# A recurrence stage of the prefix tiles issued right after its inputs instead of inside the next tile's gate stage

## The reference

```python
xn = _layernorm(x, axis=-1)
x = x + _L0_attn_ref(xn, ...) + _L0_ffn_ref(xn, ...)

# attention, 4 heads, 256 key and 512 value columns a head, per chunk:
g = log_sigmoid(xn @ Wgk1 @ Wgk2 + bgk2) / 16
bc = cumsum(g)                         # inside the chunk
qg = q * exp(bc) * scale ; kd = k * exp(-bc)
o  = tril(qg @ kd.T) @ v + qg @ S
S  = S * exp(b_last) + (k * exp(b_last - bc)).T @ v   # carried from chunk to chunk
o  = o * rsqrt(mean(o*o)) * rms_w * silu(xn @ Wg) ;  out = o @ Wo

# experts: 4 of them, the two with the best gate score are mixed per row
h = relu(_layernorm(xf @ w1 + b1)) ; y = _layernorm(h @ w2 + b2)
```

## Time and profile before

| | us |
|---|---|
| time, median of 2 runs | 2794.62 (both 2794.62) |
| time of the profiled execution | 2792.33 |
| its span on the slowest core (core 1) | 2790.8 |
| spans of all cores | 2765.2 to 2790.8 |
| PE busy | 1543.2 |
| DVE busy | 951.6 |
| ACT busy | 881.0 |
| POOL busy | 107.6 |

### The profile page before, as it was taken

How to read it: one execution, slowest core, us unless ns; L and a number is a source line. 1 busy time by engine, 2 the same in 40 slices (tenths; PEclk the granted TensorE clock), 3 DMA queues, 4 the chain that set the end, 5 groups by cost and what they waited for, 6 DMA issues and landing times.

```text
span 2790.8 us, 25315 instructions; the slowest of 8 cores (2765.2 to 2790.8 us)
## 1 busy us (share of the span) xinstructions
PE 1543.2 (55%) x6272; PEld 583.4 (21%) x6272; DVE 951.6 (34%) x2139; ACT 881.0 (32%) x1617; POOL 107.6 (4%) x152
## 2 busy tenths in 40 slices
PE   1390347316389245656965953089435656966850
PEld 0040013101134112212322311034211212322310
DVE  2433234232511233331363254430233332253253
ACT  1411361127213322313533532223413222533531
POOL 1000000000000000001010000000000000000000
PEclk9595578758699678877987975599768787988975
DMA  8041404240044310005554625223410104534323
GB/s 125 0 76 30 77 1 67 43 73 1 15 58 76 55 23 16 16 16 89 93 100 74 107 38 114 68 44 48 72 27 16 23 16 68 99 65 86 54 38 120
DMA packets 258284, 155.31 MB, mean 56 GB/s; under 512 B 173016, under 2 KB 242648, under 8 KB 258144
## 3 DMA queue, kind: packets, MB, share of 16 engines
q0 software_dynamic: 84576, 94.96, 21.6%
q1 hardware_dynamic: 168960, 41.96, 8.4%
q10 hardware_dynamic: 4608, 16.78, 1.8%
HBM read 198.04 MB, written 8.39 MB: 74 GB/s over the span
## 4 chain that ended last, share of the span: by engine, by line
PE 49%; DVE 20%; DMA 11%; issue 8%; ACT 7%; SPq 2%; DVEq 2%; ACTq 0%; POOL 0%; POOLq 0%
PE pa L291 20%; PE pb L291 19%; PE pf L291 7%; DVE s_bb L546 4%; DMA s_kgT<-s_kgs 4%; DVE s_kgs L668 2%; DMA s_gx<-x_tm 2%; DMA s_ogf<-s_ogc 2%; SPq L405 2%; ACT s_sg L470 2%; DVEq L64 2%; PE pd L291 1%; PE pc L291 1%; DVE s_z L928 1%; DVE s_z L934 1%
## 5 line engine op out<-in xcount | busy, mean ns | idle before, releaser
L291 PE MATMUL pa<-s_w,s_xn 128*128 128x512 bf16 x1280 | 328.0, 402 | 388.9 <-DVE s_v L638 236.8
L291 PE MATMUL pb<-s_w,s_xn 128*128 128x512 bf16 x1280 | 314.0, 390 | 3.9 <-DMA s_w<-W 3.9
L291 PEld LDWEIGHTS pa<-s_w,s_xn 128*128 128x128 bf16 x1280 | 124.0, 101 | 557.2 <-issue 434.7
L291 PE MATMUL pf<-s_w,s_ogf 128*128 128x512 bf16 x512 | 147.0, 458 | 123.2 <-DMA s_ogf<-s_ogc 123.2
L291 PE MATMUL pa<-s_w,s_hfm 128*128 128x512 bf16 x512 | 128.2, 396 | 74.5 <-DMA s_hfm<-s_h 64.6
L767 ACT ACTIVATE s_jb<-s_ogc 128x512 bf16<-128x512 bf16 x64 | 40.3, 629 | 394.1 <-DVE s_ogc L761 392.1
L291 PEld LDWEIGHTS pb<-s_w,s_xn 128*128 128x128 bf16 x1280 | 123.0, 100 | 165.6 <-issue 37.8
L546 DVE TENSOR_TENSOR_SCAN s_bb<-c_os,s_bb 128x128 f32<-128x128 f32 x256 | 108.8, 425 | 107.0 <-ACT s_bb L539 81.1
L848 DVE TENSOR_TENSOR s_mcol<-s_scol 128x8 f32<-128x8 f32 x16 | 2.7, 168 | 403.4 <-ACT s_jb L908 402.8
L291 PE MATMUL pb<-s_w,s_hfm 128*128 128x512 bf16 x512 | 123.0, 383 | 0.0
L668 DVE TENSOR_SCALAR s_kgs<-s_kd,s_eb 128x128 bf16<-128x128 bf16 x256 | 65.2, 255 | 167.4 <-DMA s_kgT<-s_kgs 108.8
(11 more groups left out here) (176 smaller groups left out, 2287.4 us busy)
## 6 DMA issues: line engine op xcount, KB each, us to landing
s_w<-W POOLq DMA_DIRECT2D x32, 1024.0 KB, 12.8
s_w<-Wv_p POOLq DMA_DIRECT2D x8, 1024.0 KB, 16.8
s_w<-Wv POOLq DMA_DIRECT2D x8, 1024.0 KB, 14.2
s_w<-Wg POOLq DMA_DIRECT2D x8, 1024.0 KB, 11.4
s_w<-Wo POOLq DMA_DIRECT2D x8, 1024.0 KB, 10.9
s_gx<-x_tm ACTq DMA_DIRECT2D x16, 512.0 KB, 4.2
out<-s_jf ACTq DMA_DIRECT2D x16, 512.0 KB, 2.9
s_xt<-xp_tm POOLq DMA_DIRECT2D x4, 1024.0 KB, 10.9
```

Of the source, the lines that this page charges most:

```text
L291: ret = e.matmul(out=o, lhsT=l, rhs=r, start=st, stop=sp)
```

## The change

DE of a prefix tile is no longer kept for the next tile's stage B. It is issued at the end of its own loop iteration, behind C of its tile and behind A of the next one, and so ahead of the small loads and of all of B of the next tile. `pend_pDE[0]` stays `None`, so the call of `emit_pend_pDE` in `emit_pend_G` does nothing. No operation is added or removed.

```diff
@@ -1138,7 +1138,7 @@
         cpar = cpar_of[("p", st)]
         pv = wu_next(Wv_p[:, 0:512])
         gw_ = load_B_smalls((Wgk1_p, Wgk2_p, bgk2c_p), gate=False)
-        r_ = stage_B(gw_, gate=False, xnm=xnm, epar=cpar, mid=emit_pend_pDE)
+        r_ = stage_B(gw_, gate=False, xnm=xnm, epar=cpar)
         eqm, emm = r_
         tpms, qbm_, kbm_ = stage_C(True, eqm, emm, pre=(pv, None), epar=cpar)
         sqw = [(ve, ve.n)]
@@ -1149,7 +1149,7 @@
         blks = [stage_A_blk(nsrc, nt0, b, ncp, (), sq_w=sqw)
                 for b in range(NBLK)]
         xnm = stage_A_xpose(blks, (te, te.n))
-        pend_pDE[0] = (tpms, cpar)
+        stage_DE(True, tpms, epar=cpar)
     pend_G = [None]
```

## The result

The changed kernel takes 2764.44 us (median) against 2794.68 in the same comparison. The ratio of the two is 0.9887, 95% interval 0.9874 to 0.9901, so 28 to 35 us are gained, about 1.1%. The forecast was 2765. The interval leaves out 1, so the gain is clear of the noise; under the 2% that was set as the bound, it counts as no change.

A forecast was written before the change was run, and what follows sets the result against it. The chain was half PE, otherwise split, with no engine the bound everywhere. Gains of 16.8 + 12.0 = 28.8 us off 2792.33 gave 2763.5, plus 2.3 for the median 2765.8; forecast 2765, range 2755 to 2778.

The forecast's parts named there:

- small loads: Loads ahead of B's first matmuls, now waiting for DE and lying open: 5.2 us at one place, 5.9 at the other.
- second place: DE inside B of the first main tile, with the expert gate: Ln at 682.3 against 694.3, 12.0 us gained.
- 16.8 us: Gain predicted inside B of the second prefix tile: Ln starts at 369.7 against 386.5.
- first place: DE inside B of the second prefix tile: moved ahead, it covers the wait for the transposes; 16.8 us gained.
- Ln: Activation behind DE and B's Sigmoids, taken as the mark: each us it comes earlier is a us off the end.
- cold clock: Rival: TensorE stays at 1.2 GHz in DE, 9 us more at each place, 2784; chance 0.06.
- row of the same loads: Trace row pricing the small loads' landing at 3.7 us, used instead of the skill page's about 2.0 us.
- V's quarters: Last three quarters of V's weights, issued about 344 instead of 291, landing by 365, needed at 430; costed at nothing.
- first rival: Small loads land late, sharing DMA engines with three 1 MB loads: 16.8 instead of 3.7 us, 2792; chance 0.07.
- cold groups of 3.4 and 2.7 us: Times taken for the first and second wgk1 groups on TensorE in B, behind the small loads.
- bounds of 27 to 33 us: Range of the whole gain from the bounds on small loads and second wgk1 group: 2761 to 2767.
- 24.7 us: Gain inside B of the second prefix tile from transposes ending in DE's shadow, before the price of the small loads.

The follow-up runs named there:

- e4_hold: The kernel before, DE not moved, with the second to fourth quarters of V's weights held until the transposes of xn landed; ratio 0.9833, 47 us gained.
- e3_smalls: The changed kernel with the small loads, and the first weight quarters ahead of them, issued ahead of DE; ratio 0.9827 to the kernel before.
- e8_tail: The changed kernel with V's quarters held, DE reordered by key block, its last items behind stage A and small loads ahead of them; 2662.64 us, ratio 0.9513.
- e5_after_hold: The changed kernel with V's second to fourth weight quarters held until the transposes have landed; 2745.62 us, ratio 0.9820 to the kernel before.

## Why the prediction was right, and where it saw too little

Step by step, times on the slowest core; at the second place the prediction's times are shifted by the 16.8 us that it gave to the first.

| step | predicted | measured |
|---|---|---|
| first place: first diagonal | 292.4 | 292.45 |
| DE's last copy ends | 341.3 | 342.1 |
| first matmul behind the small loads | 346.5 | 347.2 |
| second wgk1 group ends | 352.6 | 353.4 |
| Ln | 369.7 | 370.1 |
| second place: DE's last copy ends | 626.5 | 626.0 |
| gate matmuls start | 632.4 | 631.4 |
| Ln | 665.5 | 664.9 |
| span | 2762.0 | 2762.8 |

- **DE keeps its length.** 49.6 us at the first place for 48.9. The cold clock was a rival: TensorE ran at 1.2 GHz only for the first six microseconds of DE's matmuls (granted clock 0.50 from 295.4 to 301.3, 1.00 from 302.0 to 341.5). The chain has the pairs at 0.85 us before and at 0.61 after:

```profile
299.89 0.85 PE pf L291 x2
...
306.80 0.61 PE pc L291 x2
```

- **The small loads** cost 5.1 us (342.09 to 347.18) at the first place and 5.4 at the second, for 5.2 and 5.9. The row of the same loads was the right price. The chain has the landing of the last of them:

```profile
343.69 3.25 DMA s_bgk<-bgk2c_p
```

  The Trainium skill's figure of about 2.0 us fixed (DMA: Bandwidth & Descriptors, Anatomy of one DMA) would have been 1.2 us short here; the measurement decides. Without V's quarters right behind them the small loads do come near that figure. In e4_hold, with the issues from 262 to 302 as above, they landed in 2.1 and 2.2 us, while in the kernel before (280 to 318) it was 3.6 and 3.4:

```profile
s_wgk<-Wgk_p POOLq DMA_DIRECT2D x2, 32.0 KB, 2.1
s_bgk<-bgk2c_p POOLq DMA_DIRECT2D x1, 4.0 KB, 2.2
```

  So the sharing that the prediction's first rival named is there, but at 1.2 to 1.5 us and not at 13. The rule on the same page of the Trainium skill, Rules for kernel authors, that a DMA is to be issued early, held: e3_smalls got back 17 us over two places by following it. Beside the landing the open wait costs clock, which the sum had in its cold groups of 3.4 and 2.7 us (measured 3.36 and 2.89): against e3_smalls that is 1.6 us in the distance of the groups and 1.0 in the second group, half of the landing's price again.

- **V's quarters** land well ahead of their use; among the waits of the first main tile's C there is none for them, only one of 11.0 us for a quarter of Wg, which stood there before too (12.4).

- **The end follows the Ln** one to one: 29 us at the last of the two marks, 28 us at the end of the span. It also holds far beyond the forecast: in e8_tail the last mark comes 136 us earlier than in the kernel before, and the time of the profiled execution is 137 us shorter (2657.41 for 2794.62).

- **How far the close hit counts.** Each step came within about a microsecond, so the mechanism is right. That the median lies 0.6 us from the forecast is partly luck: six of the seven executions lie between 2760.75 and 2767.19. The bounds of 27 to 33 us also left out the upper bound for the small loads that stands beside them (10.5 us more at each place), which only the rival had.

- **What the prediction saw too little of** is the 24.7 us itself. It took the wait for the transposes as given and asked only how to cover it. It even said that V's loads "no longer run against the transposes" and put that at nothing, because the transposes were off the path. Right for the sum, but the collision was the cause of two thirds of the wait (some 8 of the 24.7 us are left in e4_hold): without it the Ln comes 12 to 18 us earlier at each tile, and the kernel before gains 47 us with one wait added. The stretch was legible in the profile before: at the first place one transpose held SP's queue for 1.2 us at the least and for 7.4 at the most, in the first tile for up to 8.3. The change hides, at two of three places, what a better order of the loads removes at all three, and e5_after_hold shows how little it adds then.

- **My own miss among the expectations** was the same kind of count: e4_hold was expected to give 25 us over two places and gave 47 over three.

Not tried: a hold of other large loads in the main tiles, and how the rest of the time, behind the first main tile's Ln, could be shortened.

## What to carry to other kernels

A wait that a change would cover should first be asked what made it: look at what was issued on the other queues while the awaited transfers were in flight, for a large load held back by one wait can be worth more than a stage moved. When a stage is moved ahead of loads whose waits are written as "all work issued so far", the loads move behind the stage with it, so issue them first. And an order of loops that lets a dependent chain start as its inputs land (here block by block instead of chunk by chunk) can take a whole stage off the path, provided its items don't stand ahead of work on which another engine waits.

## What the runs showed of the hardware

- Eight SBUF-to-SBUF transposes issued by SP took 15.7 to 18.2 us of its queue without V's loads in their midst (both places of the changed kernel, first tile and first place of e4_hold, all cores), 27 to 28 us with two 1 MB loads issued by GpSimd in the midst of them, and 30 to 34 us with three (second place; first place and first tile of the kernel before). The Trainium skill (DMA: Bandwidth & Descriptors, Issuing engines are not separate DMA queues) says that DMAs of SP and GpSimd run on the same 16 engines and interleave; the runs agree, and show the price. The small transfers pay and the large ones don't: at the first place the three V loads landed in 16.6 us (median) beside the transposes and in 17.8 without them.
- Small loads of 4 to 32 KB landed in 3.4 to 3.6 us with three 1 MB loads issued right behind them on the same queue, and in 2.1 to 2.2 us with these held back (first place, kernel before and e4_hold).
- Cores 0 and 1, 2 and 3, 4 and 5, 6 and 7 go in unlike pairs, before and after the change: of each pair one reaches its first Ln at 81 to 82 us and the other at 86, and the spans differ by some 10 to 23 us. Which one is later changes from run to run. The late core sets the time. What decides it stays open.
